# Inverse column transform of a spectral layer: two row tiles against two column tiles on TensorE

## The reference, cut to what matters

```
x = coords @ fc0_w + fc0_b
for sw, cw, cb in 4 layers:
    x_ft = rfft2(x, norm='ortho')
    out  = einsum('bixy,ioxy->boxy', x_ft[:, :, :20, :20], sw)
    x1   = irfft2(out zero-padded, s=(64, 64), norm='ortho')
    x2   = einsum('bchw,oc->bohw', x, cw) + cb
    x    = gelu(x1 + x2)
x = gelu(x @ fc1_w + fc1_b) @ fc2_w + fc2_b
```

## Time and profile before

| what | value |
|---|---|
| median of three runs | 1129.65 us |
| the profiled execution's own time | 1131.64 us |
| its span, first to last instruction | 1129.8 us |
| TensorE busy with matmuls (PE) | 1024.6 us, 91% |
| TensorE weight loads (PEld, beside PE) | 654.0 us, 58% |
| VectorE (DVE) / ScalarE (ACT) busy | 614.7 / 410.1 us |
| mean granted TensorE clock | 0.978 of full speed |
| `image_columns`, L1288: MATMULs | 4096, busy 266.1 us |

### The profile page before, as it was taken

One profiled execution on the slowest core, in us unless ns is written; L12 is line 12 of the kernel. 1 busy time (PEld: TensorE's weight loads), 2 busy tenths in 40 slices (PEclk: granted clock), 3 DMA queues, 4 the chain that ended last, 5 costly groups with the idle time before them and its releaser, 6 DMA issues.

```text
span 1129.8 us, 36328 instructions
## 1 busy us (share of the span) xinstructions
PE 1024.6 (91%) x16860; PEld 654.0 (58%) x16860; DVE 614.7 (54%) x773; ACT 410.1 (36%) x554; POOL 137.2 (12%) x127
## 2 busy tenths in 40 slices
PE   4899899899989999999899899889999899689996
PEld 3676567567657633676576667567325788632221
DVE  2258455825844221458248455923144577769887
ACT  2332233223223486232232233223585778421100
POOL 6000000000000000000000000020000665334421
PEclk9999999999999999999999999999999899879998
DMA  5220130022021300310220130020011000000000
GB/s 187 89 75 3 62 94 12 3 89 75 3 74 53 115 6 22 118 32 3 89 75 3 44 103 21 3 90 16 2 25 43 1 1 2 2 1 1 1 10 10
DMA packets 25660, 46.75 MB, mean 41 GB/s; under 512 B 9437, under 2 KB 10488, under 8 KB 24869
## 3 DMA queue, kind: packets, MB, share of 16 engines
q1 hardware_dynamic: 24694, 43.49, 12.6%
q10 hardware_dynamic: 384, 0.66, 0.2%
q0 software_dynamic: 432, 0.29, 0.1%
HBM read 30.25 MB, written 10.89 MB: 36 GB/s over the span
## 4 chain that ended last, share of the span: by engine, by line
PE 69%; DVE 14%; issue 6%; ACT 4%; DMA 3%; POOL 2%; SPq 1%; ACTq 0%; POOLq 0%; DVEq 0%
PE PSALL L1288 22%; PE PSALL L1256 7%; DVE WORK L1494 6%; PE PSALL L1366 4%; PE PSALL L1279 4%; PE PSALL L1232 4%; PE PSALL L517 4%; PE PSALL L1151 3%; PE PSALL L1376 3%; PE PSALL L1165 3%; PE PSALL L420 3%; DMA WORK<-MIXED 2%; PE PSALL L505 2%; DVE WORK L1513 2%; PE PSALL L399 2%
## 5 line engine op out<-in xcount | busy, mean ns | idle before, releaser
L1513 DVE STREAM_TRANSPOSE WORK<-PSALL 128x1024 f32<-128x1024 f32 x128 | 152.4, 1230 | 292.9 <-PE PSALL L1256 292.9
L1288 PEld LDWEIGHTS PSALL<-EW,WORK 64*128 64x128 f32 x4096 | 250.0, 193 | 65.5 <-issue 48.3
L1288 PE MATMUL PSALL<-EW,WORK 64*128 64x128 f32 x4096 | 266.1, 283 | 12.8 <-DVE WORK L1513 12.8
L1416 ACT ACTIVATE X<-PSALL,TABLES 128x1024 f32<-128x1024 f32 x128 | 141.7, 1114 | 331.6 <-PE PSALL L1288 331.6
L1494 DVE STREAM_TRANSPOSE WORK<-PSALL 128x1024 f32<-128x1024 f32 x84 | 102.3, 1223 | 26.8 <-PE PSALL L1151 26.8
L1397 ACT COPY SPEC<-PSALL 128x400 f32<-128x400 f32 x64 | 53.9, 851 | 152.7 <-PE PSALL L1165 149.8
L1165 PEld LDWEIGHTS PSALL<-TABLES,WORK 128*64 128x64 f32 x2000 | 67.0, 138 | 65.7 <-DVE WORK L1494 53.2
L1165 PE MATMUL PSALL<-TABLES,WORK 128*64 128x64 f32 x2000 | 80.7, 228 | 23.1 <-DVE WORK L1494 19.9
L1485 DVE STREAM_TRANSPOSE WORK<-X 128x1024 f32<-128x1024 f32 x78 | 92.8, 1207 | 16.4 <-PE PSALL L1288 16.4
L1151 PE MATMUL PSALL<-WORK,DW 32*64 32x256 f32 x2496 | 95.8, 391 | 0.0
L697 POOL MEMSET SW<- 64x4160 f32 x1 | 3.6, 3559 | 725.0 <-PE PSALL L1240 725.0
(11 more groups left out here) (156 smaller groups left out, 1059.1 us busy)
## 6 DMA issues: line engine op xcount, KB each, us to landing
SW<-in_spec_w SPq DMA_DIRECT2D x160, 80.0 KB, 2.7
spec_scr<-MIXED SPq DMA_DIRECT2D x24, 400.0 KB, 3.3
SPEC<-spec_scr SPq DMA_DIRECT2D x32, 200.0 KB
WORK<-spec_scr SPq DMA_DIRECT2D x16, 200.0 KB
WORK<-MIXED SPq DMA_DIRECT2D x64, 40.0 KB
WORK<-in_coords_w SPq DMA_DIRECT2D x2, 1024.0 KB, 4.8
XC<-in_coords_c SPq DMA_DIRECT2D x2, 1024.0 KB, 7.2
hid_scr<-WORK SPq DMA_DIRECT2D x64, 8.0 KB
```

The costliest lines, as they stand in the source:

```text
L1288: m = pe.matmul(PS[2 * p + z][:, 2 * b * GRID:(2 * b + 2) * GRID], G[64 * z:64 * z + 64, n % 2, b, h:h + 4, :, c].rearrange("p q o -> p (q ...
L1416: nc.scalar.activation(X[:, n].rearrange("p b (z d) c w -> p d z b (c w)", z=2)[:, p, :, :, 2 * t * GRID:2 * (t + 1) * GRID], PSALL[:, 2 * ...
L1513: nc.vector.transpose(G[:, n % 2, 2 * x + y].rearrange("p h o v -> p o h v"), PSALL[:, 4 + 2 * x:6 + 2 * x, :].rearrange("p k (h o v) -> p ...
```

## The change: what it does

`image_columns` still makes four matmuls with 128 moving columns. The two halves of G's partitions now hold the two pixel rows c. The matmuls contract over all 128 partitions and take 64 weight columns (two row slots h by 32 channels) instead of 128 (four by 32), in two column tiles j = 0, 1 that write the two partition halves of one bank. The two choices c are summed in one matmul by the 128 rows instead of in two matmuls one after the other. The table EW becomes block-diagonal: partitions of c = 0 carry the transform in columns 0 to 63 and zeros in 64 to 127, those of c = 1 the other way round; EW shrinks from 192 to 128 columns. The v half that is read is now chosen by t and no longer by c. To fit, the columns of the inverse row table (`inverse` in `constants`) are put in another order. Waits, semaphores, banks, and everything on the other engines stay as they are.

```diff
-        EW = sb("EW", [128, 3 * GRID])
+        EW = sb("EW", [128, 2 * GRID])
...
             def image_columns(n, t, p, b):
-                for c in range(2):
-                    h = 4 * (2 * p + t)
-                    for z in range(2):
-                        m = pe.matmul(PS[2 * p + z][:, 2 * b * GRID:(2 * b + 2) * GRID],
-                                      G[64 * z:64 * z + 64, n % 2, b, h:h + 4, :, c].rearrange("p q o -> p (q o)"),
-                                      EW[64 * z:64 * z + 64, (1 - c) * GRID:(3 - c) * GRID],
-                                      start=False, stop=True, skip_group_check=True, tile_position=(64 * z, 0))
+                for z in range(2):
+                    for j in range(2):
+                        h = 4 * (2 * z + p) + 2 * j
+                        m = pe.matmul(PS[2 * p + z][64 * j:64 * j + 64, 2 * b * GRID:(2 * b + 2) * GRID],
+                                      G[:, n % 2, b, h:h + 2, :, t].rearrange("p q o -> p (q o)"), EW[:],
+                                      start=False, stop=True, skip_group_check=True, tile_position=(0, 64 * j))
                 return m
...
-    idft_w = np.zeros((2, RI, Q, GRID))
-    idft_w[:, 0, 0:MODES], idft_w[:, 1, 0:MODES] = twice * cos.T, -twice * sin.T
+    idft_w = np.zeros((2, RI, Q, 2, GRID))
+    for c in range(2):
+        idft_w[c, 0, 0:MODES, c], idft_w[c, 1, 0:MODES, c] = twice * cos.T, -twice * sin.T
...
-        inverse = [row_of(l, 2 * half + p, q, 2 * t + c)
-                   for half in range(2) for p in range(2) for t in range(SETS) for q in range(4) for c in range(2)]
+        inverse = [row_of(l, p, q, 2 * t + c)
+                   for c in range(2) for p in range(4) for q in range(4) for t in range(SETS)]
...
-        "idft_w": np.pad(idft_w.reshape(128, GRID), ((0, 0), (GRID, GRID))).astype(f), ...
+        "idft_w": idft_w.reshape(128, 2 * GRID).astype(f), ...
```

More of the change, by code:

```diff
@@ L1621, in constants @@
         "outside": 1 - band, "band4": np.tile(band * f(HD ** -0.5), (1, 4)),
-        "idft_w": np.pad(idft_w.reshape(128, GRID), ((0, 0), (GRID, GRID))).astype(f), "ident": np.eye(128, dtype=f),
+        "idft_w": idft_w.reshape(128, 2 * GRID).astype(f), "ident": np.eye(128, dtype=f),
     }
```

## The result

The changed kernel took 1117.05 us (median of 4 runs, 1116.88 to 1123.54) against 1130.33 us for the kernel before on the same chip: a ratio of 0.9897, 95% interval 0.9860 to 0.9934. In a later set beside other variants it took 1117.79 us, ratio 0.9867 (0.9848 to 0.9886). So it gains 13 to 15 us. Forecast were 21.7 us and 1108 us; the measured time lies inside the stated range, in its upper half, and outside the 1105 to 1112 of the forecast itself.

What follows compares the result with a forecast made beforehand. TensorE was taken to bound the kernel, its column-transform rounds 10 ns longer than their MATMUL because of 128-column loads. Savings of 20.7 + 1.0 = 21.7 us from 1129.65 gave 1107.9, said as 1108 us; range 1101 to 1123.

Steps and rivals of the forecast that it cites:

- Rival C: Column-transform rounds keep 4 to 5 ns of excess, saving 0.23 us a step, 13.5 us in all: 1116 us; 22%.
- rival E: A neighbour such as VectorE work or the next group's loads takes the gain back: near 1120 us; 5%.
- Part 2: Column transform: 64-column loads vanish under the MATMUL, a round costs 107.5 ns, saving 0.37 us a step.
- Rival B: Column transform: the 10 ns belong to two-tile streams or G's stride and stay; only 3 us go: 1126.5 us; 9%.
- part 7: What could be late next: ScalarE moves along, VectorE's transposes (4.8 us) fit in 5.9, so no cost.
- Part 4: Inverse parts: seven of eight steps save in full, 56 x 0.37 = 20.7 us; the first steps add 1.0 us.
- Rival A: Column transform: loads and MATMULs on the same 128 rows exclude each other, about +80 us, 1210 us; 4%.

Runs made afterwards that it cites:

- e5: Kernel before with 64 instead of 128 moving columns in each column-transform matmul, loads still 128 columns; one run, 1144.49 us.
- e2: Kernel before with each column-transform matmul cut into two of 64 weight columns, on the column halves of the same row tile; 1112.61 us, ratio 0.9823.
- e8: Changed kernel with only the first 64 of its 128 moving columns, leaving out the second pixel row of each pair; one run, 1040.49 us.
- e6: Changed kernel with the call needing the last G transpose fifth instead of fourth (t = 0), and G's v halves laid out apart; 1163.50 us, ratio 1.0259.
- e9: Kernel before with the call needing the last G transpose made fifth instead of fourth in t = 0 steps; one run, 1133.67 us.
- e1: Changed kernel with the call needing the last G transpose made fifth instead of fourth in t = 0 steps (late fourth call); 1112.53 us, ratio 0.9817.
- e11: Changed kernel run once more as it is, in a later set beside the late fourth call with filler; 1117.79 us.
- the filler: Changed kernel with the late fourth call and one more `keep_busy` matmul ahead of layer 0's first inverse rows; 1110.07 us, ratio 0.9815.

## Why the prediction was right or wrong

**Direction and mechanism: right.** Rounds bound by loads of 128 columns, freed by loads of 64, is what e5, e2 and e8 show. The saving was over-estimated by a third (21.7 us forecast, 16.3 in undisturbed inverse parts). That the time still lies in the range is owed to the range's width: it took in rivals C and E.

**Part 2, the saving of a step (0.37 us): off by 0.05.** The round fell to 109.2 ns, not 107.5. That 1.7 ns is neither the stride (e6) nor the kind of tile (e2), for both have 109.2. The term that was mis-sized is the price of the MATMUL itself: 107.5 is a quarter of a 512-column MATMUL, and a MATMUL of 128 columns costs 109.2, as channel mixing had shown before the change. The prediction compared the mixing only by its total of 4.78 us, with two waits in it, and found no excess; the starts of its single MATMULs would have given the 109. 32 x 1.7 ns are the 0.05 us. The excess before the change was read as overhead on top of a load of 110 ns. It is 8.6 ns over the MATMUL, and 6.1 of them are the stride of the weight read: side by side the load allows 111.7. Rival B named the stride and drew the wrong end from it: it stays, but it slows a load that is no longer the limit.

**The difference of t = 0 and t = 1: misread.** The 0.07 us by which a t = 0 step was longer were put down to the four waits' own cost, "and that stay". They were the last transpose being late (e9), and so they grew to 0.18 when the columns became faster (e1). This is the step of the prediction that failed, together with part 7, which claimed that VectorE's work "fits" in a step of 5.9 us. It fits by its sum; what was not asked is when the last of it is needed: the fourth call is due 1.36 us into the columns, and the transposes end 1.43 us into them. The 64 instructions were forecast at 3.67 us (t = 1) and 3.75 (t = 0); the timeline has 3.72 and 3.89. The prediction had named a wait for VectorE in the steps as a sign of being wrong, and the row at 254.08 shows it. It is rival E's mechanism. That was given 5%, and priced at some 12 us; the change made it 0.18 - 0.07 = 0.11 us longer in 24 steps, 2.6 us.

**Part 4, the steps.** Measured per inverse part: four steps of t = 1 at 0.32, three of t = 0 at 0.21, the first step 0.10: 2.0 us, times eight 16.3 instead of 21.7. The difference is 24 x 0.16 = 3.8 us from the t = 0 steps and 32 x 0.05 = 1.6 from the others. With the late fourth call the parts sum to 20.7 us less than before (434.7 to 414.0), near what the prediction promised for the change alone.

**The rest, 16.3 to 14.8 us of span:** clock falls, which the prediction left out. Two sat in the changed kernel's inverse parts and took 2.7 us; 1.2 came back outside the inverse parts. They differ from run to run. They may make up much of the scatter (1114 to 1120 us in e11): there the shortest run has the highest mean clock (0.980) and the longest the lowest (0.975, shared with one of 1117.46), but only one run of each set was traced.

**Rival A.** The rounds of 109.2 and 60.0 ns rule it out. The rule in the Trainium skill, "TensorE: Matmul & The Clock Gate", "Part 3: Packing small matmuls — row/col tiling", that a weight load overlaps with running MATMULs only when its row group differs, does not hold for two column tiles here: e8 fits two 128-row loads and two MATMULs into 60 ns.

**Rival C** gave the time closest to the measured one (1116) for a reason that the runs do not bear out: it kept 4 to 5 ns of excess in every round, and none is left over a MATMUL of 109.2.

## What to carry to other kernels

In a stream of short matmuls compare the time of a weight load with that of the MATMUL above it, count the stride of the weight read, and take both prices from rounds of the same length. Where the load was the longer, halving its columns paid here even with twice the instructions (e2). When one engine gets faster, look for the place where its input is due the earliest, not at whether the producer's total fits. A difference of a few hundredths of a microsecond between like steps may be such a wait; here it grew from 0.07 us to 0.18 and, in e8, to 0.74. The cure was to move one call. In undisturbed inverse parts it gained 8 x 0.53 = 4.2 us on top of the 16.3 of the change, and the whole kernel took 1110 us (with the filler) to 1113 us.

## What the runs showed of the hardware that was not expected

- A float32 weight load of 128 columns read with a stride of two numbers goes with a round of 117.8 ns, side by side of 111.7 ns; the recorded durations (193 and 188 ns) hardly tell which of the two is near the MATMUL's 109.2.
- Two column tiles of 128 rows and four tiles of 64 rows by 64 columns stream at the same 109.2 ns a round with 128 moving columns, and so do four column tiles of 32 columns. MATMULs of 128, 416 and 512 columns (109.2, 349 and 429 ns) fit 0.833 ns a column and 2.5 ns each.
- A STREAM_TRANSPOSE of 128 x 1024 float32 takes 1.23 us when it writes pairs of neighbouring numbers and 1.90 us when it writes single ones.
- The stretches at half clock move from one execution of the same program to the next (44 and 450 us in one, 546 us in another); with slower transposes ahead of the first step (e6) there was one in each inverse part.
